# Layer 0's selective scan: x_proj of two opposite directions in one product, the backward rows kept in DRAM, eight of sixteen states turned, carried states copied four at a time

## The reference, cut to what matters

```python
x0 = xc.reshape(B, d, L)
x1 = jnp.transpose(xc, (0, 1, 3, 2)).reshape(B, d, L)
xs = jnp.stack([x0, x1, x0[..., ::-1], x1[..., ::-1]], axis=1)      # four directions
x_dbl = jnp.einsum('bkdl,kcd->bkcl', xs, x_proj_w)                  # 8 + 16 + 16 rows
dts_r, Bs, Cs = (x_dbl[:, :, :R], x_dbl[:, :, R:R + N], x_dbl[:, :, R + N:])
dt = jax.nn.softplus(jnp.einsum('bkrl,kdr->bkdl', dts_r, dt_proj_w) + dt_proj_b[None, :, :, None])
...
    dA = jnp.exp(dt_l[..., None] * A)
    h = h * dA + (dt_l * u_l)[..., None] * B_l[:, :, None, :]
    y = jnp.einsum('bkdn,bkn->bkd', h, C_l)
```

## Time and profile before

| | us |
|---|---|
| median of 3 runs | 7704.68 (7701.81 to 7710.51) |
| profiled execution, its span | 7975.8 |
| scan of the first image, of which all four are alike | 836.08 |
| scans of the four images in the profiled execution | 3344.77 |

### The profile page before, as it was taken

The page is one execution under the profiler, slowest core; times in us unless marked ns, Lnnn a source line. Parts: engine busy times, 40 slices in busy tenths (PEclk is TensorE's granted clock), DMA queues, the critical chain, the costliest instruction groups (busy, mean ns, idle before and its releaser), DMA issues. The chain is left out here.

```text
span 7975.8 us, 170513 instructions
## 1 busy us (share of the span) xinstructions
PE 7187.8 (90%) x62522; PEld 6186.6 (78%) x62522; DVE 5972.5 (75%) x9085; ACT 4078.3 (51%) x8541; POOL 3659.8 (46%) x4037
## 2 busy tenths in 40 slices
PE   8999899998999989999756788879988999999999
PEld 6888778886788867888546666645667989989999
DVE  7999889997899978999644555545556767767677
ACT  5888668885688757888311222224543222222222
POOL 5888658885688847888355555410000000000000
PEclk9999999999999999999878899889998999999999
DMA  2333223332233322333366555400003434434343
GB/s 66 90 93 93 75 64 92 93 90 68 74 90 93 92 58 83 90 94 90 109 174 171 164 160 152 119 4 3 0 6 95 125 116 125 125 116 128 113 129 108
DMA packets 590364, 763.42 MB, mean 96 GB/s; under 512 B 51703, under 2 KB 527896, under 8 KB 587585
## 3 DMA queue, kind: packets, MB, share of 16 engines
q1 hardware_dynamic: 537921, 585.72, 25.8%
q0 software_dynamic: 51840, 169.91, 7.5%
HBM read 721.77 MB, written 33.66 MB: 95 GB/s over the span
## 5 line engine op out<-in xcount | busy, mean ns | idle before, releaser
L647 POOL TENSOR_TENSOR l_arena<-l_arena 128x768 f32<-128x768 f32 x1536 | 2591.3, 1688 | 449.1 <-DVE l_arena L579 443.6
L579 DVE TENSOR_TENSOR_SCAN l_arena<-l_arena,psum 128x772 f32<-128x772 f32 x1536 | 2664.5, 1751 | 176.6 <-PE psum L406 72.5
L500 ACT ACTIVATE l_arena<-l_arena,l_A 128x384 f32<-128x384 f32 x3072 | 1643.7, 604 | 38.2 <-DVE l_arena L579 32.7
L408 PE MATMUL psum<-l_arena 128*128 128x128 f32 x11520 | 1499.3, 280 | 46.8 <-DVE l_arena L579 43.0
L408 PEld LDWEIGHTS psum<-l_arena 128*128 128x128 f32 x11520 | 1367.4, 192 | 170.5 <-issue 146.7
L419 PE MATMUL psum<-l_ident,l_arena 128*128 128x128 f32 x9216 | 1257.6, 273 | 50.6 <-ACT l_yT L506 41.7
L419 PEld LDWEIGHTS psum<-l_ident,l_arena 128*128 128x128 f32 x9216 | 1055.2, 141 | 60.2 <-POOL l_arena L647 60.2
L2269 POOL TENSOR_TENSOR st_mab<-st_xr 128x384 f32<-128x384 f32 x8 | 7.8, 1000 | 2053.1 <-DVE st_xr L2259 2053.1
L1211 POOL DMA_INDIRECT l_G<-neighbours,l_idx x648 | 621.2, 959 | 650.2 <-PE psum L1259 301.0
L490 ACT ACTIVATE l_arena<-l_arena,l_BT 128x256 f32<-128x256 f32 x1728 | 747.0, 496 | 7.5
L2544 ACT ACTIVATE st_own_s<-psum 128x384 f32<-128x384 f32 x256 | 125.7, 491 | 1092.5 <-PE psum L2381 1092.5
(11 more groups left out here) (436 smaller groups left out, 11291.5 us busy)
## 6 DMA issues: line engine op xcount, KB each, us to landing
l_arena<-c_rows SPq DMA_DIRECT2D x1536, 192.0 KB, 3.1
st_FS<-filter_sums SPq DMA_DIRECT2D x128, 1155.0 KB, 9.2
st_F<-filter_parts SPq DMA_DIRECT2D x128, 320.5 KB, 7.2
neighbours<-l_xt SPq DMA_DIRECT2D x256, 72.0 KB
st_mab<-in_st_mp SPq DMA_DIRECT2D x68, 256.0 KB, 9.5
st_mab<-in_st_mm SPq DMA_DIRECT2D x68, 256.0 KB, 6.2
l_G<-neighbours,l_idx POOLq DMA_INDIRECT x648
l_arena<-in_x SPq DMA_DIRECT2D x4, 1152.0 KB, 5.2
```

The costliest lines, as they stand in the source:

```text
L408: mm = pe.matmul(ps[:, o:o + P], dtuT[:, g % 2, t, h * P:(h + 1) * P], diagB[:, rank[s] % 3, t, :], start=True, stop=True)
L500: act.activation(decay[:, s % NDC, half(h)], dtv[:, g % 2, h, :], ACT.Exp, scale=A[:, g // NRC, h, n:n + 1]).then_inc(s_exp, 1)
L579: dve.tensor_tensor_scan(hbuf[:, n, run], decay[:, s % NDC, run], x2_ps[s % 2][:, run], 0.0, ALU.mult, ALU.add).then_inc(s_scan, 1)
L647: pool.tensor_tensor(hC[:, s % NHC], halves(hbuf[:, s % NS, :]), Cs[:, s % NCS, :].unsqueeze(1).broadcast_to([P, 2, RC]), ALU.mult).then_i ...
```

## The change

- x_proj of directions k and k+2 of the same chunk is one product, whose weights have 105 columns (40 rows, a row of ones, a gap, 40 rows and a row of ones). It is made in the forward groups only, its two halves (h = 0, 1) in slots 0 and 1 instead of both in slot 0. ACT copies all 105 rows, with a bias operand that lays the two rows of ones.
- SP stores the 41 rows of the opposite direction to a new DRAM tensor `back_rows`. In the backward groups there is no product and no copy: SP loads the 41 rows, and the C rows are broadcast from `back_rows`.
- The later slots of the preparation move one slot back (delta to 3 and 6, softplus to 4 and 7, and so on); delta_u of POOL moves from step 7 to 8.
- TURNED has eight states instead of six.
- The decays have eight slots instead of four; POOL's carry copies four slots in one instruction, after every fourth step, five to eight steps ahead.

```diff
-NCS, NDC, NHC = 6, 4, 4
+NCS, NDC, NHC = 6, 8, 4
+DG = 4
+NROW = 64 + RK + 2 * NS + 1
+KEPT = RK + 2 * NS + 1
+FWD = 2 * NRC
-TURNED = (2, 5, 7, 10, 12, 15)
+TURNED = (2, 4, 6, 8, 10, 12, 14, 15)
...
-                    def store_C(g):
+                    def store_rows(g):
                         sp.wait_ge(s_lo, g + 1)
                         if g >= 2:
                             sp.wait_ge(s_hc, NS * (g - 1))
+                        k, c = place(g)
                         sp.dma_start(c_rows[g % 2], low[NS:2 * NS, g % 2, :]).then_inc(s_cw[g % 2], 16)
+                        sp.dma_start(back_rows[k, c], low[64:64 + KEPT, g % 2, :]).then_inc(s_cw[g % 2], 16)
+                    def load_rows(g):
...
+                        sp.wait_ge(s_dtp, 2 * (g - 2) + 2)
+                        sp.wait_ge(s_btp, g - 1)
+                        k, c = place(g)
+                        sp.dma_start(low[0:KEPT, g % 2, :], back_rows[k, c]).then_inc(s_lr[g % 2], 16)
...
+                        if s % NS == 0 and FWD <= g + 1 < NCH:
+                            load_rows(g + 1)
...
-                    def rows(g):
-                        if g:
+                    def rows(g, h):
+                        if g >= FWD:
+                            return
+                        if g and h == 0:
                             pe.wait_ge(s_tc, 2 * g)
...
+                        mm = pe.matmul(ps[0:NROW, work:work + RC], xp_w[:, g // NRC, h, :], inputs(g, h), start=(h == 0), stop=(h == 1))
...
                     def delta(g, h):
                         if h and g:
                             pe.wait_ge(s_dt, 2 * g + 1)
+                        elif g < FWD:
+                            pe.wait_ge(s_lo, g + 1)
                         else:
-                            pe.wait_ge(s_lo, g + 1)
+                            pe.wait_ge(s_tc, 2 * g)
+                            pe.wait_ge(s_lr[g % 2], 16 * ((g - FWD) // 2 + 1))
...
-                        act.activation(low[0:RK + 2 * NS, g % 2, :], ps[0:RK + 2 * NS, work:work + RC], ACT.Copy).then_inc(s_lo, 1)
+                        act.activation(low[0:NROW, g % 2, :], ps[0:NROW, work:work + RC], ACT.Identity,
+                                       bias=row_ones[0:NROW, 0:1]).then_inc(s_lo, 1)
...
-                        dve.wait_ge(s_cr, s + 1)
+                        dve.wait_ge(s_cr, s // DG + 1)
...
-                            ins = pool.tensor_copy(pair(decay[:, s % NDC, :], at), pair(hbuf[:, n, :], end))
+                            ins = pool.tensor_copy(ends(slots, at), ends(hbuf[:, n:n + DG, :], end))
...
-                        if s + 3 < NSTEP:
-                            carry(s + 3)
-                        if s % NS == 7 and s // NS + 1 < NCH:
+                        q = (s + 1 + NDC - DG) // DG
+                        if s % DG == DG - 1 and q * DG < NSTEP:
+                            carry(q)
+                        if s % NS == 8 and s // NS + 1 < NCH:
```

More of the change, by code:

```diff
@@ L142, in layer0 @@
         s_nil, s_cr = scan_sem("nil_columns"), scan_sem("carried")
-        s_cw = [scan_sem(f"C_rows_stored_{r}") for r in range(2)]
+        s_cw = [scan_sem(f"rows_stored_{r}") for r in range(2)]
+        s_lr = [scan_sem(f"rows_loaded_{r}") for r in range(2)]
         s_cl = [scan_sem(f"C_laid_{r}") for r in range(NCS)]
@@ L336, in _, with place @@
                 def _(sp):
-                    def store_C(g):
+                    def place(g):
+                        return g // NRC % 2, chunk(g)[1].start // RC
+                    def store_rows(g):
                         sp.wait_ge(s_lo, g + 1)
@@ L358, in rows @@
                             pe.wait_ge(s_tc, 2 * g)
[L359 to L362, removed]
+                        mm = pe.matmul(ps[0:NROW, work:work + RC], xp_w[:, g // NRC, h, :], inputs(g, h), start=(h == 0), stop=(h == 1))
+                        if h:
+                            mm.then_inc(s_rows, 1)
@@ L424, in project @@
                     def project(g, slot):
-                        if slot == 0:
-                            rows(g)
-                        elif slot == 2:
+                        if slot < 2:
+                            rows(g, slot)
+                        elif slot == 3:
                             delta(g, 0)
-                        elif slot == 5:
+                        elif slot == 6:
                             delta(g, 1)
-                        elif slot == 8:
+                        elif slot == 9:
                             turn_B(g)
@@ L588, in project @@
                     def project(g, slot):
-                        if slot == 4:
+                        if slot == 5:
                             delta(g, 0)
-                        elif slot == 7:
+                        elif slot == 8:
                             delta(g, 1)
@@ L620, in delta_u, with ends, carry @@
                         ins.then_inc(s_du, 1)
-                    def pair(row, o):
-                        return row[:, o:o + RC + 3:RC + 2]
-                    def carry(s):
+                    def ends(rows, o):
+                        return rows[:, :, o:o + RC + 3:RC + 2]
+                    def carry(q):
+                        s = q * DG
                         n, g = s % NS, s // NS
@@ L630, in carry @@
                         end = half(0).start if back else half(0).stop - 1
+                        slots = decay[:, s % NDC:s % NDC + DG, :]
                         if s % (NSTEP // 2) < NDC:
-                            pool.memset(pair(decay[:, s % NDC, :], zero_at), 0.0)
+                            pool.memset(ends(slots, zero_at), 0.0)
                         if g % NRC == 0:
-                            ins = pool.memset(pair(decay[:, s % NDC, :], at), 0.0)
+                            ins = pool.memset(ends(slots, at), 0.0)
                         else:
-                            ins = pool.tensor_copy(pair(decay[:, s % NDC, :], at), pair(hbuf[:, n, :], end))
+                            ins = pool.tensor_copy(ends(slots, at), ends(hbuf[:, n:n + DG, :], end))
                         ins.then_inc(s_cr, 1)
                     delta_u(0)
-                    for s in range(3):
-                        carry(s)
+                    for q in range(NDC // DG):
+                        carry(q)
                     for s in range(NSTEP):
@@ L2661, in program @@
         c_rows = nc.dram_tensor("c_rows", (2, NS, RC), F32, kind="Internal").ap()
-        layer0(nc, x_in, part("l0_"), x1, c_rows)
+        back_rows = nc.dram_tensor("back_rows", (KD // 2, NRC, KEPT, RC), F32, kind="Internal").ap()
+        layer0(nc, x_in, part("l0_"), x1, c_rows, back_rows)
         with nc.sbuf_tensor("stream", [P, NT], F32) as stream:
```

55 lines of the change are left out of this document (35 added, 20 removed).

## The result

| | before | after |
|---|---|---|
| median of the runs, us | 7703.69 (7701.81 to 7710.51, 4 runs) | 7836.69 (7832.21 to 7854.79, 4 runs) |
| four scans, us | 3344.8 | 3259.7 |
| layer 0, first to last instruction, us | 3919.0 | 3828.2 |
| layer 3's spectral part (its function's lines), us | 2001.7 | 2222.5 |

The ratio is 1.0174, with a 95% interval of 1.0159 to 1.0188: slower by 1.7%, where 1.2% faster was forecast. The four scans lost 85.1 us, and layer 0 as a whole 90.8, where 92 was forecast for the scans. Code that the change does not touch, in layer 3, took 220.8 us more.

The account below looks back on a forecast made before the run. No engine was full: a group was DVE's own work plus what PE's preparation pushes into it. Per image 0.5, 3.8, 4.3 and 14.4 summed to 23.0 us, 92 in four, so 7704.7 became 7613; range 7545 to 7682.

Parts of the forecast that it names:

- the last of the sum: Whole kernel: the unprofiled run loses the same 92 us as the profiled scans, 7704.7 to 7613.
- The sum of the groups: Scans: plain forward groups 34.3 us, those without a product 32.5, backward 33.3; 23.0 us less per image, 92 in four.
- Two diagonals fewer: DVE, from two more turned states: 2 x 0.45 = 0.9 us per group, if DVE is waited for.
- The wide product: PE's x_proj product with 105 columns: 0.35 us a pass taken, 0.45 the other end, adding 16 us.
- The copy's bias operand: ACT's row copy before keep_y: 0.12 us more for the bias operand.
- Rival A: Scan engines stop waiting for each other; groups fall to DVE's 31.2 and 32.1 us, 7399 us in all; chance 0.10.
- its lesser form: POOL's carry: its 39.4 us of idle time before scans is won, 7574 us; most of A's 0.10 chance.
- Rival B: Forward groups lose what backward ones win, keep_y another 2.2 us late in ten groups: 7700 us; chance 0.09.
- Rival C: ACT becomes the scan's bound, its instructions not overlapping: 115 us slower, 7820 us; chance 0.06.
- Rival D: Backward groups: SP's loaded rows come 3.1 us late for PE's delta, 149 us slower, 7762 us; chance 0.05.
- The profiled execution: Whole kernel: profile before, 7975.8 us, is 271 us longer than the unprofiled run; forecast to go to 7884.

Follow-up runs that it names:

- place 71: Changed kernel with 60 more instructions at the start of PE's program, so layer 3's loop starts at instruction 71 modulo 256: 7617.09 us.
- place 159: Changed kernel with 148 more instructions at the start of PE's program, putting layer 3's loop where it lay before the change: 7633.32 us.
- its own run: Kernel before with only eight decay slots and POOL's carry of four states at a time: 7710.37 us, ratio 0.9999.
- the run with delta ahead: Changed kernel, 60 more PE instructions, eight turned, on PE delta ahead of the sum that waits for keep_y: 7562.92 us.
- place 11: Loop's place in the changed kernel, 7836.69 us; kernel before moved there by 108 more PE instructions: 7937.62 us.

## Why the prediction was wrong, point by point

- **The step that failed** is the last of the sum: "I expect the unprofiled run [...] to lose the same: 7704.7 - 92 = 7613". It takes everything outside the scan as fixed. The scan lost what it should, but 660 instructions fewer on PE moved layer 3's loop to a place where it is fetched again in every turn, 221 us. No rival had such a mechanism: all four lay inside the scan. With the loop at place 71 the same change takes 7617, 4 us from the forecast, and at place 159, where the loop stood before, 7633, 20 us from it. The closer hit is in part luck: the scans lost 82 us there, not 92, and a few us outside them came on top.
- **The sum of the groups** held: 34.1, 32.8 and 33.3 against 34.3, 32.5 and 33.3. The scans as a whole lost 85 us of 92; the 12 long groups took about 12 x 1.2 = 14 back, which the prediction did not know of. The groups that prepare direction 1 take 35.4 against 35.6, the long ones left out.
- **"Two diagonals fewer" at 0.9 per group, if DVE is waited for:** it is not. With six turned the backward groups are the same and the forward ones 0.8 shorter, so the two more turned states cost 40 us here, 16 long groups of 1.2 among them. The prediction priced them inside one chain together with the moved slots and came out even; alone, one part wins 1.0 and the other gives 0.8 back.
- **The wide product** was to lie between 0.35 and 0.45 a pass. Half of it holds PE for 0.65 (194.21 to 194.86), less than the 0.71 that was taken, so the wider weights do not hold PE longer. The estimate of 54 ns more for a weight load of 105 columns than for one of 40, from the Trainium skill (page "TensorE: Matmul & The Clock Gate", section "LDWEIGHTS (loading the stationary operand)"), is what the loads themselves show: their median is 171 ns after and 117 before (PEld, L389 and L361). But they run beside products, and the sum that the prediction worked out from it, 9 us less gain, does not show.
- **The copy's bias operand** was taken at 0.12: 0.58 against 0.49, so 0.09.
- **Rival A:** its lesser form (carry) is refuted by its own run, the rest by groups of 34.1 and 33.3, not 31.2 and 32.1. **Rival B:** keep_y did not come 2.2 later than forecast, but at 7.8 instead of 8.1; ACT's chain to it did matter, since delta standing behind it cost 1.0 a group (the run with delta ahead). **Rival C:** ACT waits 1.82 at the row copy and is busy 31.1 of 34.1. **Rival D:** no delta waits for the loaded rows; all 2.7 us of idle time ahead of delta's 384 products are ACT's.
- **The profiled execution** of before, 271 us too long, was rightly set aside, though its reason was not known: 264 us of the surplus were in layers 1 and 2.

## What to carry to other kernels

A change in the number of instructions on an engine moves every later loop on it: after such an edit compare the untouched stages too, and where one grew, look for idle time that "issue" ends and for more packets on the instruction queue; some idle instructions ahead of the loop, at more than one count, tell (here 24 cured nothing and 60 did). Test the parts of a bundle one by one: here the gain came, by elimination, from the product left out and from the slots that moved, while carry and split gave nothing and the turned states took time away. An engine relieved of work that nobody waits for may lose its clock.

## What the runs showed of the hardware that I had not expected

- PE's loop of 1669 instructions costs nothing after its first turn at places 71, 75 and 159 of a block, and it costs 9.3 us and 9 packets of 16.4 KB a turn at place 11 (9 packets too at 35); at 200 it is brought in once more, in the second turn. The Trainium skill, page "Runtime: NRT & Kernel Launch", section "Instruction fetch mechanics", says that a taken branch outside a window of two pages (of 16 KiB) forces a fetch, and that crossing a block is mostly hidden. The stall behind the jump agrees with the first; but a loop over six and a half blocks that runs without any fetch has no room in two pages, so the measurement decides.
- With pauses of PE of 0.2 to 0.5 us in a group, the granted clock fell to 0.50 in some groups and not in others that read alike; with six states turned it fell in none. What sets the groups apart stays open.
